# A two-layer decoder on one core: layer-norm small work on POOL, fewer products in the bias, row sums and weight folds, and the order laid in 30 passes

## What is computed

```python
x = _layernorm(x + _L0_attn_ref(x, ...))     # x @ (Wr + Wc) + bias, triangular decay matrices
x = _layernorm(x + _L0_xattn_ref(x, ctx))    # causal cross attention, 16 heads of 16
x = _layernorm(x + _L0_ffn_ref(x, ...))      # 8 experts, one per token, plus a shared one
x = _layernorm(x + _L1_attn_ref(x, ...))     # FFT per head, prefix sum over rows
x = _layernorm(x + _L1_xattn_ref(x, ctx))    # latent cross attention, 16 heads of 128
x = _layernorm(x + _L1_ffn_ref(x, ...))      # ternary weights, rms norm of the hidden row

def _layernorm(x, eps=1e-05):                # over the last axis
    return (x - mean(x)) / sqrt(var(x) + eps)
```

## Time and profile before

| | |
|---|---|
| runs of the kernel, us | 691.98 median of 3, 689.49 to 692.77 |
| the profiled execution, us | 693.77, of which the span is 692.5 |
| PE busy | 590.3 us, 85% |
| DVE busy | 506.3 us, 73% |
| ACT busy | 406.3 us, 59% |
| POOL busy | 362.0 us, 52% |
| mean granted TensorE clock | 0.938 of full speed |
| chain that ended last, by engine | PE 55%, DVE 21%, ACT 8%, waits of issue 5% |

### The profile page before, as it was taken

How to read it: one execution, slowest core, us unless ns; L and a number is a source line. 1 busy time by engine, 2 the same in 40 slices (tenths; PEclk the granted TensorE clock), 3 DMA queues, 4 the chain that set the end, 5 groups by cost and what they waited for, 6 DMA issues and landing times.

```text
span 692.5 us, 14605 instructions
## 1 busy us (share of the span) xinstructions
PE 590.3 (85%) x5393; PEld 456.3 (66%) x5393; DVE 506.3 (73%) x1297; ACT 406.3 (59%) x914; POOL 362.0 (52%) x405
## 2 busy tenths in 40 slices
PE   3899989889689999935448789999988999999995
PEld 3566867668566566622126578898666777878885
DVE  2675667668667666757999878678698998968475
ACT  2667756767665454624534637665855666577474
POOL 2255345364753003269899894635654544256465
PEclk9899999999999999965867999999998999999998
DMA  6753221110535432441101010001100010000001
GB/s 190 211 162 107 55 92 48 52 41 2 168 117 166 142 104 84 123 151 50 40 25 56 1 32 1 2 1 31 32 26 6 1 31 3 1 1 2 1 1 62
DMA packets 50416, 41.98 MB, mean 61 GB/s; under 512 B 15513, under 2 KB 48794, under 8 KB 50330
## 3 DMA queue, kind: packets, MB, share of 16 engines
q1 hardware_dynamic: 48810, 36.85, 17.9%
q0 software_dynamic: 1536, 4.20, 1.9%
HBM read 31.72 MB, written 10.35 MB: 61 GB/s over the span
## 4 chain that ended last, share of the span: by engine, by line
PE 55%; DVE 21%; ACT 8%; issue 5%; SPq 4%; DMA 4%; POOL 3%; DVEq 0%; POOLq 0%
PE bank L1032 8%; PE bank L1034 8%; PE bank L1033 8%; PE bank L1039 7%; PE bank L1453 6%; SPq L858 4%; PE bank L1217 2%; PE bank L1120 2%; PE bank L1106 2%; DVE wide L1766 2%; DMA wide<-in_L_ffn_down_w 2%; ACT first L1592 1%; PE bank L1129 1%; PE bank L1318 1%; DVE wide L1869 1%
## 5 line engine op out<-in xcount | busy, mean ns | idle before, releaser
L1766 DVE TENSOR_TENSOR first<-bank,first 128x512 f16<-128x512 f32 (+3 forms) x141 | 75.6, 556 | 23.3 <-ACT first L1601 9.8
L1039 PE MATMUL bank<-c_identity,first 128*128 128x128 f32 (+2 forms) x353 | 60.0, 285 | 23.5 <-DMA first<-in_x 9.8
L2223 POOL TENSOR_TENSOR first<-first 128x512 f16<-128x512 f32 x44 | 51.2, 1164 | 42.7 <-ACT first L1653 35.8
L1039 PEld LDWEIGHTS bank<-c_identity,first 128*128 128x128 f32 (+2 forms) x353 | 39.7, 140 | 35.0 <-ACT first L1592 10.3
L1032 PE MATMUL bank<-wide,first 128*128 128x256 f16 (+3 forms) x199 | 55.8, 290 | 4.5 <-DVE first L1766 2.1
L1039 PE MATMUL bank<-c_identity,wide 128*128 128x128 f32 (+3 forms) x211 | 36.6, 297 | 26.1 <-POOL wide L2311 9.0
L1033 PE MATMUL bank<-wide,first 128*128 128x256 f16 (+3 forms) x199 | 55.8, 290 | 0.0
L1034 PE MATMUL bank<-wide,first 128*128 128x256 f16 (+3 forms) x199 | 55.7, 290 | 0.0
L2203 POOL TENSOR_TENSOR first<-first,minus_half 128x2 f32<-128x2 f32 x30 | 22.2, 739 | 55.5 <-DVE first L1875 55.5
L1039 PEld LDWEIGHTS bank<-c_identity,wide 128*128 128x128 f32 (+3 forms) x211 | 24.7, 147 | 33.1 <-POOL wide L2311 10.1
L2258 POOL TENSOR_TENSOR wide<-wide 128x768 bf16<-128x768 bf16 x8 | 13.5, 1685 | 61.1 <-DVE wide L1862 61.0
(11 more groups left out here) (469 smaller groups left out, 2160.0 us busy)
## 6 DMA issues: line engine op xcount, KB each, us to landing
first<-sent_rows SPq DMA_DIRECT2D x20, 128.0 KB, 2.0
made_rows<-first SPq DMA_DIRECT2D x20, 128.0 KB, 1.9
wide<-in_L_xattn_Wq SPq DMA_DIRECT2D x9, 256.0 KB, 3.1
wide<-in_L_ffn_gate_w SPq DMA_DIRECT2D x8, 256.0 KB
wide<-in_L_ffn_up_w SPq DMA_DIRECT2D x8, 256.0 KB
wide<-in_L_ffn_down_w SPq DMA_DIRECT2D x8, 256.0 KB
wide<-in_L_xattn_Wo SPq DMA_DIRECT2D x16, 128.0 KB
wide<-in_L_ffn_w_gate_up SPq DMA_DIRECT2D x8, 256.0 KB
```

What stands on the lines that cost most here:

```text
L1039: last = nc.tensor.transpose(view[0:m, c0:c0 + n], src, kc["identity" if dt == F32 else "identity_bf"][0:n, 0:n])
L1766: return V.tensor_tensor(lo, whole, hi, ALU.subtract)
L2223: G.tensor_tensor(B.pl[r], B.pf, B.ph[r], ALU.subtract).then_inc(says("ex_l"), 1)
```

## The change

The norm's small operations leave DVE and ACT and become four instructions of `ln_pow` on POOL, with two waits of POOL on itself between them. The bias becomes one product with all 128 rows, of which two carry the halves and the others are zero. Row sums: POOL adds the two halves of the squares once more (128 by 256) after the last group, and PE makes two products in place of four. Folds: one turning in place of two; the four products of `hb` alternate between result rows 0 to 63 and 64 to 127; the keys' matrix `krT` is laid out with two blocks on its diagonal, in a buffer zeroed once, so that `hc` makes two full products in place of four half ones. The lengths given to the planner change with them, and the order is laid 30 times.

```diff
     def norm(u, n, rank, summed="res"):
-        p.add("ln", u, n, "DVE", 131, [(summed, u, n)], rank)
-        p.add("ln_pow", u, n, "POOL", 71, [("ln", u, n)], rank)
-        p.add("ln_x", u, n, "ACT", 120, [("ln_pow", u, n)], rank)
+        p.add("ln", u, n, "DVE", 108, [(summed, u, n)], rank)
+        p.add("ln_pow", u, n, "POOL", 95, [("ln", u, n)], rank)
+        p.add("ln_x", u, n, "ACT", 85, [("ln_pow", u, n)], rank)
...
-    p.settle(8, 8)
+    p.settle(8, 30)
...
     def hb(u, j):
...
-        for n in range(HEADS):
-            for q in range(2):
-                last = mm(b[0:R, n * D:(n + 1) * D], W.qr[:, q, n, :], k.t1[:, n, q, :], start=(q == 0), stop=(q == 1))
+        for q in range(2):
+            for n in range(HEADS):
+                last = mm(b[n * R:(n + 1) * R, 0:D], W.qr[:, q, n, :], k.t1[:, n, q, :], start=(q == 0), stop=(q == 1))
...
     def hc(u, j):
...
-            for n in range(HEADS):
-                mm(b[:, (2 * c + n) * DC:(2 * c + n + 1) * DC], k.t2[:, n * D + c * P:n * D + (c + 1) * P], k.krT[:, n * DC:(n + 1) * DC],
-                   start=True, stop=True)
+            mm(b[:, c * P:(c + 1) * P], k.t2[:, c * P:(c + 1) * P], k.krT, start=True, stop=True)
...
-                    for half in range(2):
-                        last = mm(o, kc["all_ones"][0:1, :], k.bias[half], start=False, stop=(half == 1))
+                    last = mm(o, kc["all_ones"], k.bias, start=False, stop=True)
...
     def rm(u, g):
...
-            for n in range(2):
-                last = mm(b[:, t:t + 1], B.ss[:, n * S + t * P:n * S + (t + 1) * P], k.one, start=(n == 0), stop=(n == 1))
+            last = mm(b[:, t:t + 1], B.ss[:, t * P:(t + 1) * P], k.one, start=True, stop=True)
...
     def hk_c(u, j):
-        fn(k.krT, bank("hk", 0, j)[0:R, 0:HEADS * DC], ACT.Copy).then_inc(says("hk_c"), 1)
+        act.wait_ge(*done("pm_pow", 0))
+        for n in range(HEADS):
+            own = slice(n * R, (n + 1) * R)
+            last = fn(k.krT[own, n * DC:(n + 1) * DC], bank("hk", 0, j)[own, 0:DC], ACT.Copy)
+        last.then_inc(says("hk_c"), 1)
...
     def ln_x(u, n):
...
-        for t in range(T):
-            last = fn(B.shift[:, t:t + 1], B.mean[:, t:t + 1], ACT.Copy, scale=B.rstd[:, t:t + 1])
-        act.step(last)
...
     def ln(u, n):
...
-        dve.step(last)
-        V.tensor_scalar(B.mean, B.mv[:, :, 0], -1.0, None, ALU.mult)
-        V.tensor_scalar(B.rstd, B.mv[:, :, 1], EPS, None, ALU.add).then_inc(says("ln"), 1)
+        last.then_inc(says("ln"), 1)
...
     def ln_pow(u, n):
...
-        G.tensor_tensor(B.rstd, B.rstd, k.minus_half, ALU.pow).then_inc(says("ln_pow"), 1)
+        G.tensor_scalar(B.mean, B.mv[:, :, 0], -1.0, None, ALU.mult)
+        pool.step(G.tensor_scalar(B.rstd, B.mv[:, :, 1], EPS, None, ALU.add))
+        pool.step(G.tensor_tensor(B.rstd, B.rstd, k.minus_half, ALU.pow))
+        G.tensor_tensor(B.shift, B.mean, B.rstd, ALU.mult).then_inc(says("ln_pow"), 1)
...
     def ss(u, g):
...
-        G.tensor_tensor(B.ss, B.ss, B.s1, ALU.add).then_inc(says("ss"), 1)
+        last = G.tensor_tensor(B.ss, B.ss, B.s1, ALU.add)
+        if g == 3:
+            pool.step(last)
+            last = G.tensor_tensor(B.ss[:, 0:S], B.ss[:, 0:S], B.ss[:, S:2 * S], ALU.add)
+        last.then_inc(says("ss"), 1)
```

More of the change, by code:

```diff
@@ L609, in program @@
     k.w_fp = sb("w_fp", [P, FH // P, D], BF16)[:]
-    k.bias = pair("bias", [1, D])
+    k.bias = sb("bias", [P, D], F16)[:]
     k.slot_of = sb("slot_of", [P, NW])[:]
@@ L673, in program @@
     pre.dv = wide.tile([2])
-    pre.bias = wide.tile([S], F32, 1)
+    pre.bias, pre.rest = wide.tile([S], F32, 2), wide.tile([S], F32, 2)
     pre.ones32 = wide.tile([P])
@@ L1096, in hk @@
         W = k.W[k.stage_no["h", j] % 2]
-        flip(bank("hk", 0, j), [(n * DC, R, W.kr[:, n, :]) for n in range(HEADS)]).then_inc(says("hk"), 1)
+        flip(bank("hk", 0, j), [(0, P, W.kr.rearrange("p h n -> p (h n)"))]).then_inc(says("hk"), 1)
     def ha(u, j):
@@ L2190, in pm_b @@
     def pm_b(u, g):
-        pool.step(G.tensor_copy(k.bias[0], pre.bias))
-        G.tensor_tensor(k.bias[1], pre.bias, k.bias[0], ALU.subtract).then_inc(says("pm_b"), 1)
+        rows = k.bias[0:2, :]
+        pool.step(G.memset(k.bias, 0.0))
+        pool.step(G.tensor_copy(rows, pre.bias))
+        pool.step(G.tensor_scalar(pre.rest, rows, kc["identity"][0:2, 1:2], None, ALU.mult))
+        G.tensor_tensor(rows, pre.bias, pre.rest, ALU.subtract).then_inc(says("pm_b"), 1)
     def eg_lo(u, e):
```

27 lines of the change are left out of this document (14 added, 13 removed).

## The result

The changed kernel took 683.24 us, median of four runs (681.7 to 684.47), the kernel before 690.82 beside it: ratio 0.9887, 95% interval 0.985 to 0.9924. So it is faster by 7.6 us, where 24 were forecast. The profiled execution took 682.36 us, its span 681.1.

A forecast was written before the change was run, and what follows sets the result against it. PE was taken to bound the kernel, except from 300 to 400 us, where DVE and POOL are fuller. Six terms summed to 23.8 us off 693.8, giving 670.0, lowered by 1.8 to 668; range 655 to 685.

The forecast's parts named there:

- Rival 1: Start of layer 1: ternary turn 5 holds the first gather, layer 0's 10.6 us waited away; 679 us; chance 0.15.
- Rival 3: Norms: POOL's four instructions blocked by DVE, a norm takes 2.2 us against 1.83; about 680 us; chance 0.12.
- Bias and folds, the sizes: Layer 0: `hb` saves 0.71 us, query products 0.28, one turning 0.10 per fold; bias 0.30 saved, 16 times.
- Bias and folds, on the path: Layer 0: savings multiplied by PE's busy share (0.89, about 0.91): bias 2.7 us, folds 7.9 us.
- Row sums: Tail of each unit: half the products save 0.48 us, eight times, times 0.93: 3.6 us.
- My own clause: Row sums: POOL's add lies beside PE's work of other units; uncovered, as in the last unit, the tail is even.
- Norms, the chain: Statistics to normed rows: 0.3 us shorter, 12 times where PE sat idle: 3.6 us, bounds 0 and 7.2.
- Norms, the engines: From 300 to 400 us: DVE loses 6.5 us of work, POOL gains 3.6; counted as 2 us gained.
- Order: Start of layer 1: 16, not 11, ternary POOL instructions before the first gather move 8.2 us; half counted, 4 us.
- Rival 2: Start of layer 1: `x_mid` loads start 22 us late behind turn 6's load; slower, 701 us; chance 0.05.
- Rival 4: Start of layer 1: new order removes half of PE's 43 idle us from 300 to 400; 653 us; chance 0.08.
- What would show it: Right: `hb` 1.1 to 1.2 us, PE below 575, norm's way 1.3 to 1.6, gather 290 to 300; wrong: 305 or later.

The follow-up runs named there:

- e2: Instructions of the kernel before, laid in the changed kernel's order (new lengths, 30 passes): 681.34 us, ratio 0.9848 to the kernel before.
- e1: All instructions of the changed kernel, laid in the order of the kernel before: 700.51 us, ratio 1.0133 to the kernel before.
- f1: Changed kernel with the norms of the kernel before, in the changed kernel's order: 677.41 us, ratio 0.9783 to the kernel before.
- e4: Kernel before with only the products changed (bias, folds, row sums), in the old order: 689.33 us, ratio 0.9969 to the kernel before.
- e3: Kernel before with only the norms changed, in the old order: 705.25 us, ratio 1.0201 to the kernel before.
- h3: f1 with the folds of the kernel before, same order: 681.43 us, ratio 0.9861 to the kernel before.
- h4: f1 with the row sums of the kernel before, same order: 675.06 us, ratio 0.9771 to the kernel before.
- h1: g2 with two idle POOL operations added behind each norm's signal: 673.33 us, ratio 0.9722 to the kernel before.
- h2: g2 with one small ACT operation added ahead of each norm's normed rows: 672.58 us, ratio 0.9735 to the kernel before.
- i2: g2's instructions, layer 0 laid by the old order's urgencies, layer 1 and ternary turns by the changed kernel's: 681.12 us, ratio 0.9838 to the kernel before.
- j1: g2's instructions, old lengths, 8 passes, gathers forced behind turn 5's last ternary operation: 685.62 us, ratio 0.9904 to the kernel before.
- g2: Changed kernel, same order, norm shared: DVE adds eps and makes minus the mean, POOL root and product: 669.67 us, ratio 0.969 to the kernel before.

## Why the prediction was half right

The direction and the range held; the size did not. That the time lies in the range is partly luck: norms and products came out 22.5 us worse than their terms and the order 6.5 better, and the upper end of the range was taken from rivals 1 and 3, not from the forecast's own terms. Two steps failed: the norms, priced as a gain, are a loss, and the products' saving was multiplied by PE's busy share as if it reached the end. The sum, with each term's measured worth (order first, then products, then norms, so that they add up to the whole: 0.9848, 0.9783, 0.9887):

| term | forecast | measured |
|---|---|---|
| order | 4, up to 8.2 | 10.5 (e2); 17.0 if it is taken last (e1 to changed) |
| bias, folds, row sums | 2.7 + 7.9 + 3.6 = 14.2 | 4.5 (e2 to f1), uncertain by 3; 2.1 in the old order (e4) |
| norms | 3.6 + 2 = 5.6 | -7.2 (f1 to changed), uncertain by 3; -13.9 in the old order (e3) |
| together | 23.8 | 7.8 |

- **Bias and folds, the sizes.** Right or low. `hb` saved 0.86 for 0.71 forecast, near the upper bound; the query products 0.49 for 0.28. PE had 13.5 us less to do up to the first gather in `e4`, which is the 4.8 + 8.7 of the forecast before it left out the first 40 us and multiplied by the busy share.
- **Bias and folds, on the path.** This step failed. I multiplied by PE's busy share (0.89, 0.91), as if PE worked through layer 0 without waiting for anything. In the old order 11.1 of the 13.5 us became idle time of PE. In the new order more came through: the folds gave 5.4 (`h3`), of a term of 7.9. Being 89% busy does not mean that the last 9% of the work can be taken away for gain.
- **Row sums.** The loads fell from 0.97 to 0.52 as forecast by the rows. But the end did not move (`h4`). My own clause, that an uncovered add of POOL costs about what the products gave, may hold more widely than I took it, but the trace shows it in two of the eight units only, where the loads wait for line 2336 for 0.25 and 1.45 us. By the rule of the Trainium skill (TensorEngine Tiling (Array Packing), section Instruction Overhead) the term would have been 0.8; that is nearer to nothing, but its price of 25 ns does not agree with the loads, 0.11 us less for each load left out. (The 0.8 takes each of the 32 records left out as a product; by the 16 products it would be 0.4.)
- **Norms, the chain.** This step failed. POOL's small operations take 0.29, 0.31 and 0.23 from start to start where 0.15, 0.32 and 0.18 were counted, so the way of the last norm is 1.69 and not 1.54. The norm was also priced by one typical way, 1.83 before; over all 48 the ways before come to 133.1 us, 2.8 each, where 48 times the last norm's 1.59 would be 76: the rest is waits and blocking. With the new norms in the same order they rose to 139.2 (`e3`). The 0.24 of blocked line 1874 was won for the most part: 17 of its 48 operations took over 0.1 us longer than the shortest, 11.7 us in all; of POOL's first two operations 5 and 4 did, 4.3 us in all. In layer 1's first norm the blocking is there, 0.93, 0.53 and 1.02 for three of them. By the rule of the Trainium skill (SBUF — State Buffer, section SBUF: two separate sides) the one that starts first holds the shared port pair and the other blocks (of DVE's operations those in a two-port mode or, as this one, with two inputs in SBUF); the trace agrees, as POOL's operation ends 0.09 us after DVE's. PE's waits for normed rows, 14.7 us before, did not shrink either: 17.5 in `e3`, and 19.2 in the changed kernel besides the one of 17.04 that goes with the order. And in `e3` 10 of 12.9 us came as more busy time of PE at a lower granted clock, which no term had.
- **Norms, the engines.** This step failed too. DVE did get its relief from 300 to 400 us (75.9 busy, 84.2 before), but POOL is at 88.3% there as before although five ternary instructions moved ahead, since each norm costs it four operations where it had one: from `f1` to the changed kernel POOL is busy 33 us more, 0.7 for each norm. I set the two engines against each other as a gain of 2; at the start of layer 1 the runs show a loss, 346 records for 381 in `e3` and 458 for 488 of `f1`, with DVE freer in both. Rival 3 (chance 0.12) had the sign and nearly the size, 12 above the forecast; measured against the forecast's term the norms are 12.8 worse (5.6 gained, 7.2 lost). Its mechanism, POOL blocked by DVE in four operations, is a small part of it by the 4.3 us above. What makes up the rest, POOL's time or the way, is open (`h1`, `h2`).
- **Order.** Right in place, low in size. In `e2` PE does more in the first 100 us of layer 1, and its clock rose with it, from 0.74 to 0.85. That second gain I had not priced: of the 19.2 us that layer 1 is shorter, 10.7 are less busy time at a higher clock. Nor does the whole gain come from the ternary instructions that I counted (`i2`, `j1`). What I did not see at all is that the same order ends layer 0 later, by 11.9 us in `e2`.
- **Rival 1** named the symptom: the first gather at 306.89, layer 0's gain waited away, layer 1's kept. With 679 it came nearer than the forecast. Its cause is wrong, though. Turn 5 had ended 2.81 us before; the gather waited for the experts' last store: the new order ends layer 0 later (317.4 in `e2`), and the new products bring that back to 307.8 (`f1`). Rival 2 did not happen: the `x_mid` loads began at 307.62, right behind the load of turn 6. Rival 4, the order giving more, was right in its direction: `e2` lies 6.5 us beyond the 4 that were counted, of the rival's 15, and the norms took it back. Its mechanism, half of PE's idle time at the start of layer 1 gone, did not happen: in the first 100 us PE is idle 36.2 us in `e2` and 41.5 before.
- **What would show it.** Of the right signs `hb`, the bias, the row sums' loads and PE's 569.4 us below 575 were there. The first gather after 305 was the wrong sign, and the norm's way stood at 1.69 against the bound of 1.6.

## What to carry to other kernels

Where a planner or list decides the order, measure the instructions and the order apart: lay the new instructions in the old order and the old ones in the new. Here the order alone moved one kernel by 25 us, and hid that one part of the change cost 7 to 14 us. What a part is worth also depends on the order it is measured in: the shared norm gave 6 to 8 us in one and nothing in the other. Before pricing work taken from an engine by its busy share, ask what waits end its short idle times. When small operations move to another engine, count them start to start with their handovers, and ask which engine is the fuller where it matters; sharing them, so that only those that must wait for each other stand in line (`g2`), was the best of the three here.

## What was not expected of the hardware

- The fp32 products of 96 x 256 with results in the two halves of the rows take 1.01 us for four (eight records), where four into one half took 1.87: 54% of the time for the same columns. The place of the results changed, and with it the order of the four; which of the two does it was not tested.
- An operation of two columns costs POOL 0.20 to 0.23 us of its own and about 0.3 from one to the next that waits for it; one of DVE's takes 0.17.
- The same products in the same order took 10.0 us more of PE's time in `e3` than before, with PE only 2.9 us longer idle; the granted clock of layer 1 went from 0.92 to 0.90. In these two executions the changed norms cost more by the clock than by the wait.
